# Cross-attention and quantized FFN on one core: three reorderings at the end of attention

## The reference

```python
x = x + xattn(layernorm(x), ctx)        # 16 heads of 32, rotary q and k, softmax over 120 keys
x = x + ffn(layernorm(x))

def xattn(q, c):
    q, k, v = q @ Wq, c @ Wk, c @ Wv
    attn = softmax(rope(q) @ rope(k).T / sqrt(32))
    return (attn @ v) @ Wo

def ffn(x):                             # act_qdq: 16-bit levels over the largest |value| of the whole tensor
    x = act_qdq(x)
    up, gate = act_qdq(x @ dq(w_up).T), act_qdq(x @ dq(w_gate).T)
    return act_qdq(act_qdq(gate * sigmoid(gate)) * up) @ dq(w_down).T
```

## Time and profile before

| what | value |
|---|---|
| median of 3 runs | 2301.62 us (2297.78 to 2309.82) |
| the profiled execution | 2301.44 us, span 2299.6 us |
| PE busy | 2195.2 us, 95% of the span, 12037 instructions |
| DVE, ACT, POOL busy | 1688.6, 1330.0, 709.4 us |
| DMA | 500.14 MB, 287190 packets, queue q1 68.9% of 16 engines |
| granted PE clock, mean | 0.987 |

### The profile page before, as it was taken

One profiled execution on the slowest core, in us unless ns is written; L12 is line 12 of the kernel. 1 busy time (PEld: TensorE's weight loads), 2 busy tenths in 40 slices (PEclk: granted clock), 3 DMA queues, 4 the chain that ended last, 5 costly groups with the idle time before them and its releaser, 6 DMA issues. The chain is left out here.

```text
span 2299.6 us, 31161 instructions
## 1 busy us (share of the span) xinstructions
PE 2195.2 (95%) x12037; PEld 968.4 (42%) x12037; DVE 1688.6 (73%) x1690; ACT 1330.0 (58%) x1299; POOL 709.4 (31%) x655
## 2 busy tenths in 40 slices
PE   6898999999988899999999999999997899999999
PEld 3443333333333444444444444444443344444444
DVE  7657998898975676545433698888888877778773
ACT  3346666666644223223322887878786877777772
POOL 3555666675653211001100453444443000000000
PEclk9999999999999999999999999999999899999999
DMA  6345777787887677889775898778786465565552
GB/s 194 104 118 132 174 190 180 185 182 181 179 161 180 188 219 252 250 258 280 245 229 200 282 332 303 280 285 302 281 300 230 184 238 223 225 238 207 203 212 92
DMA packets 287190, 500.14 MB, mean 217 GB/s; under 512 B 187980, under 2 KB 190284, under 8 KB 250172
## 3 DMA queue, kind: packets, MB, share of 16 engines
q1 hardware_dynamic: 287036, 498.10, 68.9%
HBM read 247.75 MB, written 186.58 MB: 189 GB/s over the span
## 5 line engine op out<-in xcount | busy, mean ns | idle before, releaser
L1708 PE MATMUL banks<-XB,W 128*128 128x512 f16 x2304 | 499.0, 380 | 2.3 <-ACT XB L1734 2.3
L1708 PE MATMUL banks<-XB,WT 128*128 128x512 f16 x2304 | 497.4, 379 | 0.0
L2174 PE MATMUL banks<-W,OH 128*128 128x512 f16 x2256 | 488.8, 380 | 2.4 <-DVE OH L2276 2.4
L1728 ACT ACTIVATE OB<-banks,uns 128x512 f32<-128x512 f32 x384 | 255.7, 684 | 390.6 <-PE banks L1708 387.9
L1708 PEld LDWEIGHTS banks<-XB,W 128*128 128x128 f16 x2304 | 225.7, 98 | 275.2 <-issue 3.6
L1708 PEld LDWEIGHTS banks<-XB,WT 128*128 128x128 f16 x2304 | 225.4, 98 | 271.8
L2174 PEld LDWEIGHTS banks<-W,OH 128*128 128x128 f16 x2256 | 221.1, 98 | 270.1 <-DVE OH L2276 2.9
L1995 POOL TENSOR_TENSOR PR<-GS,OB 128x2048 f32<-128x2048 f32 x46 | 220.7, 4797 | 257.4 <-ACT OB L1728 247.5
L1817 DVE TENSOR_REDUCE amx<-OB 128x1 f32<-128x2048 f32 x48 | 109.7, 2285 | 238.2 <-ACT OB L1728 238.2
L703 PE MATMUL banks<-XD,WQ 128*128 128x512 f16 x768 | 178.9, 383 | 10.3 <-ACT QE L1008 8.6
L762 PE MATMUL banks<-XC,AH 128*128 128x512 f16 x768 | 178.9, 384 | 5.0 <-POOL AH L1520 3.6
(11 more groups left out here) (272 smaller groups left out, 2867.5 us busy)
## 6 DMA issues: line engine op xcount, KB each, us to landing
g_s<-OB SPq DMA_DIRECT2D x48, 1024.0 KB, 6.0
GL<-g_s SPq DMA_DIRECT2D x48, 1024.0 KB, 7.4
up_s<-OB SPq DMA_DIRECT2D x48, 1024.0 KB, 4.9
XA<-up_s SPq DMA_DIRECT2D x32, 1024.0 KB, 9.4
gq_s<-GQ SPq DMA_DIRECT2D x48, 512.0 KB, 4.7
XD<-gq_s SPq DMA_DIRECT2D x48, 512.0 KB, 6.7
XA<-in_x SPq DMA_DIRECT2D x16, 1024.0 KB, 6.3
QW<-QE SPq DMA_DIRECT2D x128, 128.0 KB, 3.1
```

What stands on the lines that cost most here:

```text
L1708: t = e.matmul(pk[:].rearrange("p (j t) -> p j t", j=4), WT[w][:, ot, wa, kk, :], XB[i % 2][:, xa, :, kk, :], start=(kk == 0 and wa == 0 a ...
L1728: e.activation(OB[n % 3][:, r, :], bank[(k + 4) % 8][:], ACT.Copy, scale=uns[:, 12 * w + ot:12 * w + ot + 1]).then_inc(s_ev, 1)
L2174: t = e.matmul(pk[:].rearrange("p (r n) -> p r n", r=4), OH[i % 2][:, a, ot, j * 128:(j + 1) * 128], WD[:, :, c, wa, o4, :], start=(ot == ...
```

## The change

1. On PE, in steps 64 and above the output projection stands between scores and largest; before, it stood behind largest.
2. On SP, eleven of the twelve transpositions of gate weights go to steps 24, 28, 32, 40, 44, 48, 52, 56, 57, 60 and 64, the last stays behind the steps. Their waits are relaxed to the group of keys that each overwrites (scores of 16, 32 or 48 units done).
3. On SP, the two x1 loads go from step 64 to step 66.

```diff
+GATE_TURN = (24, 28, 32, 40, 44, 48, 52, 56, 57, 60, 64)
...
         def sp_gate_turn(e, t):
-            e.wait_ge(s_c1, 48)
+            e.wait_ge(s_c1, 16 if t <= 2 else 32 if t <= 6 else 48)
...
-                if s >= 57:
-                    sp_gate_turn(e, s - 57)
-
-                if s == 64:
+                if s in GATE_TURN:
+                    sp_gate_turn(e, GATE_TURN.index(s))
+
+                if s == NSTEP - 1:
                     for i in range(2):
...
                 if u == NU - 4:
-                    sp_gate_turn(e, NO - 2)
                     sp_gate_turn(e, NO - 1)
...
+                if s >= NU:
+                    for u in output_at(s):
+                        pe_output(e, u)
                 if 0 <= s - 2 < NU:
                     pe_largest(e, s - 2)
...
-                for u in output_at(s):
+                for u in output_at(s) if s < NU else []:
                     pe_output(e, u)
```

## The result

| | before | after |
|---|---|---|
| median | 2304.96 us (2297.78 to 2311.56, 7 runs) | 2318.92 us (2313.18 to 2325.36, 7 runs) |
| span of the profiled execution | 2299.6 us | 2317.1 us |
| ratio after/before | | 1.0067, 95% interval [1.005, 1.0084] |

The prediction said 2302.7 us, 2289 to 2314, with 0.75 on no change that can be measured. The changed kernel is slower, and outside the range.

What follows compares the result with a forecast made beforehand. The prediction took the DMA queue to set the pace in the middle of attention, with PE 2.3 us slack per window. 2301.4 + 9.8 - 2.5 - 6.0 = 2302.7 us, no measurable change; range 2289 to 2314.

Steps and rivals of the forecast that it cites:

- part 1: Middle of attention: seven transpositions between the first RB pair and the load of x cost 1.4 us each, 9.8 us.
- the loop of loads: Middle: statistics, reciprocal, first RB, issue of the x load, statistics again; 38.2 us, said to set the four-step window.
- Over 2.5 us: Sign for rival B: windows from step 24 to 52 grow by more than this.
- rival B: Middle: SP can't get rid of a transposition, 2.6 us each, 18.2 together; total 2311.1 us, or 2317; chance 0.20.
- Part 2: Steps 60 to 63: one transposition remains of four; a gain of 2.5 us, with ends at 0 and 3.5.
- Part 3: End of attention: PE's new order and the moved x1 loads gain 6.0 us, with ends 0 and 9.8.
- MX's 0.4 us: Steps 64 and 65: DVE's maxima, no longer the exponential, end PE's wait; 0.4 us charged for each step.
- RB's 6 us to POOL: Step 65: the second pair of RB takes about 6 us from issue to POOL, where it took 11.7.
- start 5.4 us earlier: Projection 52 at attention's end: AH ready at 707.0 in place of 712.39, a gain of 5.4 us.
- 0.6 us gained for the projection: Projection behind the wait for AH: 4.01 us, not 2.76; with a shorter wait half the difference counted as gain.
- Rival A: Middle: the transpositions are hidden, part 1 is 0; total 2292.9 us, at the far ends 2288.1; chance 0.25.
- Rival C: End: the x1 loads collide at their new place, ahead of batch 14's sums; part 3's gain goes, 2308.7 us; chance 0.10.

Runs made afterwards that it cites:

- turn_after_swap: Changed kernel with each transposition one step later, between that step's swap and the second pair of RB; 0.9995 against the kernel before, middle 353.1 us.
- wait_swap: Changed kernel, but in steps behind a transposition SP waits for the swap to land before issuing the second RB pair; 1.0094 against the kernel before, middle 372.3 us.
- rb2_after: Changed kernel with only the second pair of RB of each batch read by four DMAs of one row each; 0.9893 against the kernel before, middle 332.0 us.
- copies_small: Kernel before plus a 256 KB load in 2048 pieces of 128 bytes in seven steps, 24 to 52; 1.008 against the kernel before, middle 360.4 us.
- turn_c3: Changed kernel with the transpositions in the last step of each four (27, 31, ... 63); 0.9964 against the kernel before, middle 345.5 us.
- copies: Kernel before plus a plain 256 KB load of a stored weight tile in seven steps, 24 to 52; 1.0015 against the kernel before, middle 342.0 us.
- end_only: Kernel before with PE's new order and the later x1 loads, transpositions as before; 1.0006 against the kernel before, middle 339.6 us.
- copies2: Kernel before plus a plain 512 KB load (half a batch of x) in seven steps, 24 to 52; 1.0055 against the kernel before, middle 354.6 us.
- spread_only: Kernel before with only the moved transpositions and relaxed waits, PE's order and x1 loads as before; 1.008 against the kernel before, middle 368.5 us.
- rb16_after: Changed kernel with each RB read by four DMAs of one row each; 0.9843 against the kernel before, middle 325.6 us.
- copies_late: Kernel before plus a plain 256 KB load and six tiny DMAs behind it in seven steps, 24 to 52; 1.0031 against the kernel before, middle 349.9 us.

## Why the prediction was wrong

**The step that failed is part 1.** It charged seven transpositions at 1.4 us, all through the loop of loads (bounds 0 and 14.7 us), which made 9.8; the middle lost 24.8. As a price of the loop the 1.4 was good: turn_after_swap, where the loop alone pays, has 1.5 each. What the step left out is a second way to PE. It listed what is queued behind the transposition on SP (swap, second pair of RB, XD, load of x) and followed only the last to its waiter. The swap has a waiter too: POOL's rotation product, with AH behind it, ACT's A and QE behind that, and PE. In the profile of before that chain ended no wait in the middle, so it had no row among those I read, and the sum had no term for it. It had room for 1.4 us, but not for 5. And the swap isn't late by the transposition's own time: behind the same transposition its second half lands after 6.1 us where RB waits (wait_swap), 5.5 where RB is four DMAs (rb2_after), and 10.6 where RB, on a quarter of the engines, is right behind.

I had part of the row for it. The earlier trace rows gave the share of 0.27, and I used it only to ask whether the transposition could hide beside RB, not what happens to a short DMA that has to share those engines with RB. The other part was in the trace, but not among the rows: the swap of step 29 landed in halves, after 2.7 and 5.4 us, with the second pair of RB behind it.

**The signs.** Windows were to grow by about 1.4 us with DVE's wait for x grown by as much: they grew by 6.9 and 4.9 in steps 28 and 32, and not at all in step 24, and that wait fell, from 11.5 to 4.1 us in the middle. The window from step 36 was not to grow; it fell by 2.6 (38.44 to 35.82). "Over 2.5 us" was the sign for rival B, and in time B was nearest, 2311 to 2317. But its mechanism, SP that can't get rid of the transposition, is at most a small part of what the changed kernel shows. SP's 3.30 us do push the swap of step 29 back, by 1.5 us against the start of step 28. But the swaps of steps 45 and 57 are issued 1.6 and 2.3 us earlier than before, counted in the same way, and are held up all the same; and wait_swap, whose swaps are issued as late or later in seven of the eight steps, has waits for QE of 0.94 us at most in the middle. (copies_small shows B's mechanism nearly pure, at 2.5 us a window, with pieces of 128 bytes.) That B's number came nearest was luck.

**The slow clock** was in no term. After each new wait PE ran below its full clock, 0.79 in step 30; in the window from step 28 that is 38.02 - 35.83 = 2.2 us more of busy time for the same matmuls.

**Part 2** was right: one transposition left, -3.5 us where 2.5 was taken and 3.5 was the end. turn_c3 has 35.82 there, PE's own time. But the size of this gain hangs on the one trace of before: copies, end_only and copies2, with this stretch as before, have 45.89, 45.51 and 44.93 us, since the hold-up strikes in step 62. Against such an execution the gain would be some 6 us more.

**Part 3**: the mechanism was right, the size too large. It said that the moved loads decide and that PE's order is worth little by itself; measured 5.3 and 0.8 us, each with the other edit in place. MX's 0.4 us and RB's 6 us to POOL came as predicted, the latter in part by luck: POOL had other work up to there. The projection was to start 5.4 us earlier against step 64 and did so by (712.39 - 680.13) - (728.73 - 701.24) = 4.8. The term that was mis-sized is the clock behind it: I counted 0.6 us gained for the projection (4.01 us before), but it took 5.28, 1.3 lost. With PE's old order the wait for AH is only 0.52 us and the projection takes 2.75: an early PE waits longer and then runs slower. Against that, with the old order the projections of steps 64 and 65 take 4.45 and 7.04 us where turn_c3 has 2.76 and 5.35, and the two waits for the exponential are back. What is left of both is the 0.8.

**Rival A** (the transpositions are hidden) is out by spread_only, though the first window of the changed kernel behaves so; with RB spread over the engines it comes true (rb16_after). **Rival C** didn't happen: the x1 loads landed in 7.3 to 9.2 us and DVE's reciprocal of batch 14 had no wait for RG.

## What to carry to other kernels

When a transfer is moved in a queue, follow every DMA behind it to whoever waits for it, not only the one that closes today's loop: a short, urgent transfer between a long one and one that uses few engines is the one that gets hurt. Look at each small DMA's time to landing and at what stands right behind it, not at the median; two halves of a swap that landed 3.3 us apart were in the profile of before. And when a share of a few tenths stands beside a queue that bounds the kernel, mend that transfer first: splitting RB's read was worth about 30 us, where the three places tried for the transpositions, with the end's edits in all three, gave ratios of 0.9964 (turn_c3), 0.9995 (turn_after_swap) and 1.0067, some -8 to +15 us.

## What was not expected of the hardware

- Two halves of a swap issued 0.6 us apart landed 5.8 us apart (5.4 and 10.6 us after their issue), with a DMA transposition ahead of them and a pair of RB behind. Without the pair behind, they took 5.9 and 6.1; with the pair as four DMAs each, both took 5.5. In two of eight such steps (25 and 49) the halves landed together even with the pair behind; why, no run shows. The Trainium skill, page "DMA: Bandwidth & Descriptors", section "Queues, rings and completion order", has each engine take descriptors in ring order, lets a later one finish its write before an earlier one, and lets the semaphore's write land only after that engine's earlier writes. The first and the last leave no room for RB to hold a swap issued ahead of it, the second does; 10.6 against 5.9 to 6.1 us says that here it is held. Whether the swap's data or its semaphore is late, no trace shows.
- The same 256 KB cost SP 0.61 us to issue in pieces of 128 bytes, and then 6.52 us at the next DMA; as a transposition 3.30 us; in long pieces 0.4 to 0.45.
- The hold-up in step 62, with the same order in the steps around it, is 0.36 us in the profile of the kernel before and 0.32 in copies_late, and 5.86 to 6.2 in end_only, copies, copies2 and copies_small. In the first two the swap's second half lands after 4.5 and 4.7 us, in the other four after 10.0 to 11.7. What decides it stays open.
- After 3 to 5 us without work PE's granted clock was 0.79 over the long step, and one group of 8 matmuls took 1.94 us in place of 1.06. Shorter waits did it too: in the kernel before, two waits of 2.17 us stand ahead of the 24 matmuls at 692.38, which took 7.04 us at a granted clock of 0.76.
